# A macaron layer on one NeuronCore: the hand-written orders of five engines and the PSUM banks laid out anew

## The chip, the cores and the metric

The kernel runs on one NeuronCore of a Trainium2 chip. The metric is the device time of one execution in microseconds (us). The engines are TensorE (PE; its weight loads are shown apart as PEld), VectorE (DVE), ScalarE (ACT), GpSimd (POOL) and SyncE (SP), which issues the DMAs.

## What is computed

A half step of a mixture of experts, an attention with low-rank keys and values, and a second half step of the same mixture, each on layer-normed tokens: 4 batches of 1024 tokens, 128 features, 8 experts of which the best two count, 8 query heads on 2 key heads.

```python
def ffn(tokens):                       # router_w (8,128), expert_weights (8,128,128)
    probs = softmax(tokens @ router_w.T + router_b)
    top_p, top_i = top_k(probs, 2)
    w = top_p / (top_p.sum(-1) + 1e-10)
    y_all = einsum('nh,ehd->ned', tokens, expert_weights)
    return (w[..., None] * y_all[top_i]).sum(1)       # then divided by the sum of w
def attn(x):                           # causal, scale 128**-0.5
    q = x @ wq;  k = (x @ wk_down) @ wk_up;  v = (x @ wv_down) @ wv_up
    return softmax(mask(q @ k.T) * scale) @ v @ wo
x = x + 0.5 * ffn(layernorm(x))
x = x + attn(layernorm(x))
x = x + 0.5 * ffn(layernorm(x))
```

## The kernel before

The 4096 tokens are 8 chunks of 512 (two to a batch) and 32 tiles of 128 in each half step, so there are 64 tiles of expert work. The attention of a batch is 4 quads, one for each query chunk and key head, and it goes in slots of 512 score columns: 72 a batch, 288 in all. Every engine runs one long list of steps, written out by hand as a string; one letter is one step, and the n-th time that a letter occurs is the n-th step of its kind. Semaphores carry the order between engines, so a string sets when a step goes and not what it computes. In `PE_ORDER` (line 188) a digit behind a letter is the PSUM bank that the step writes; the loop at line 253 works out from that, for every use of a bank, which earlier use it must wait for (`HOME`; `release`, line 1144, makes the waits). Banks 2 and 3 take scores once the scores have begun, bank 4 takes the weighted values.

The letters, by engine:

- PE: X, x, z transpose a chunk of normed tokens (first half step, attention, second half step); L and l are the router products; Y is half a tile of expert products (three matmuls of 512 columns); K, Q, W project keys, queries and values; M is a block of scores made only to find the row maxima; R turns a quad's maxima into a row; S is a slot of scores; V multiplies weights with values, with the denominators in the same step; J is the output projection of a tile, joined into a chunk; P, U and u prepare weights.
- ACT: E is the exponential of a score slot, C scales one of the first four experts' outputs of a tile (line 734), N, n, m standardise a tile (line 705), X, x, z, K, Q, W, R and O copy from PSUM.
- DVE: M reduces a block of maxima, C adds one of the last four experts (line 991), G is one of 23 steps of routing a unit (line 943), X, x, z take statistics, N, n, m reduce them, I and i make the low part of a transposed chunk, D is one of three steps on denominators, J adds the attention to its input.
- POOL: F is one of three steps that finish a tile of experts (lines 619, 623, 626), N, n, m are one of seven steps of a norm (line 594), A is one running sum of weights over key tiles (line 648; only quads of the second chunk of a batch have them), Y is the product that normalises a quad (line 635).
- SP: K, Q and R stack parts of keys, queries and maxima by DMA, L loads a chunk, O stores one.

Routing and norms of the half steps go by units of one or two chunks: chunk 0, chunk 1, chunks 2 and 3, 4 and 5, 6 and 7 in the first; 0 and 1, 2 and 3, 4 and 5, 6, 7 in the second. The end is thus a chain on the last chunk: V, D, Y on POOL, J, statistics, norm, z, i, l, 23 steps of G, and four tiles of C and F, and a store.

A tile's scaling on ACT and its adding on DVE wait for the tile two before it to be finished on POOL; a slot's exponential waits for the running sums that read the slot 16 before it; V's last group of a quad waits for the quad's sums.

Of the kernel before, what the change touches and what calls it, by code (L numbers as in the profile page):

```python
# [187 lines left out]
PE_ORDER = steps(
    "uX6uL7PPY2X3Y6Y5L3PY7Y2Y6Y5Y7Y2Y6Y5PY7Y3Y2UY6Y5Ux7Q2K3Q1W0X6x5M7M2M3X1L6M7M2M3LM0M1M5M7M2Q3Y0M1W5M7Q5K2M1Y3R"
    "5M7Y5M1M7M1Y6M0SY7SSY1M5M6SY0M5SY7SM1M6SY5M0M1SSM6M0R5V1M5M6M7M0SSY5M6SM7M0SVVM6M7SM0Y5SM6Y7Y0M6SM5VM7SSM6M5"  # L190
    "M1M7V6M5M0SSM1M7Y5Y0R1VM1M5M7VVSSM1x0SY5M6SM7SM1Q0SSK6M7M1SVSM5SM7M0SQ1M5SM6VSM7M0M5SJ6JM7SM0SM5VVSM7SM1M0M5"
    "SM7SJJM1SM0SM5M7W1R0SSVSM5SM0x6M7SM5X0M1SM7V5VSM1M7SX0M6SM1SVL7LSSM6Q0R5SSM1VSK6M0SSM5VM1SY0SY6M5SSW1VVM7SM5"
    "M0SY6M7SY5M1SM0SY7SM6M1SM0SM6Y1M7M0SSM6VV5VM7M0M6SSM7VM0SM6M7SQ5R1SM0SV6M7SJ5JJJM1SSY0M7M1SSM5Y7M1VSM0SY5SM1"
    "SM7M0SY1SVVM7SR0M5V6SM7M0Y5SM1Sz7Y0VVVM7SY5SM1SY6SM0M7Sz1M0SM7Vl5lSM1Y0M7SSJ1JSM7SJJSM7Y6SM1M7SVVSx1M0SM7SM6"
    "Q0SM1M7K6Q1VVM0SY6SM1SM7W0X1M5SY7SR5Y0SM5M7V6SM1SM5Y7VVM1M5M7SSx0Y6M1Y5M0M7Y1Y6SSY5M0M7SM1Y6SY0K7X1Y5M6SVL1L"
    "Y7M0SSQ6SY0SM5VVSR5M7Q6Y0SSM5W7Y6M5Y7SM0VSM5Y1M6SM0SY5SY6M7M1SM0SY7SM1Y5SR0M1VM6M1SSM5M7M0SY6M1SM5M7SY0SM1M5"
    "SV6VVM7SM1SM5Y0SSM6Y7Y1SM5SM6Y0M5SSJ6JJJM5M7SM1M6V5VVVM7M1R6SSY0M5M6SM7M1Y5Y6Y7SSM0M1V0M5Sz6SM1M5SVVVM1SM6SM"
    "5x7z0M1M6SSK7SM5l0lM1SSQ6VVM5SSJ6JSM1SM5JJSSY7M1SQ5VM1SY0M6SM5SY1M6SM5SY7SM6SW5R0SM6VVM5SY7M1SM6SM0Y5SM1M6SV"
    "0VSY1M7SSM6VSM7Y5Sx0M1SM6M5SM0SQ7R1M6SSK5VVSM0Y1SSM5M6Y0VVSM7SM5Y6SM7SM1M5M0SVM7SM1SY5SM0M7Q6R1M0SSY7M0SM6M5"
    "SM0SM1Y6SM5SY0M1SM5SY7SM1M5M6SV1VVSM5SM6M1M7SV5M0SM6M1SM7J0JJJM6SSM1M7M0VR6SM1SM6SM7VVSM0M1SM6M7SV0SSM1M5z6S"  # L200
    "z7M1SM5SVl1lSM6M7SM5VVM6SSW7SM5Y0SSM7M6VVSSM5J7JSM6SJJM5M1SM6SY7SY5SY1R6SY0VSSVSSVSY7SSY5SY6SSV1SSY0VSSVSSz7"
    "Y5SSVSSVl7SSVSSVSSVSSV1VVY0Y6Y2Y5Y3J1JJJY0Y6Y2Y5Y1Y3Y7Y0z6Y2l1Y5Y6Y3Y7Y0Y2Y1Y5"
)
DVE_ORDER = (
    "XXXXNNwwXwXwXXwNwwNIwHGGGGGGGGGGGGXGXGXGXGXGIXGXGXGGNGNGCGGCGCGGCGGGGCCCCGGGGCGCGCGCGGCGGGCGCCGxxCxCCCxnnCPX"
    "CPCPCCCCCPxCCPCCXxxXPxPnnQXKXQXIXMMMIMGGMGMGGMGMGMGMGMGGGMGGQGQGMGRGMGGGMGMGKCMCCCCMCCCMMCCCCMMxMMMCMCXRMCCM"
    "MMMMCxCxCMMMCMMMMxCCCCMMDMnMnNMNMMMMMBCCCDRCMMDMDxMDxMCCMMDMCCMQxMMKMMMxMMMMMnQnMMMXMMMMMBMMRJXMMMMMXMMIMMMI"
    "DMXGGGMDQGzGGRGGGGGGMGMKMMGGGGGGGGGGMCzCCCMMMMzCCMMMMMCMCDCMzMCXMCMMxMXMDXCXDMMNDMQRMxMMJzMMCzzzMMmCmCCMMMNB"
    "MxDMDCRxnCMCCMMDnCCiMCDCDMDMMMCCixCMMMMGGGGMCJMGCGGGMCCxMGCMGMMGzGMxGQGGGKGQGxnGnMGMGGMGMMBCCCRCIMMMCCMCCDMM"
    "MMCCCCMCMCCCMMMCCCCCIKMGCCGMGGGCGGGGMCzGCQGCCGGRGMQGMGGGGGMCCGCGGCMDMCMCCCMMMCCCMMCxCCMCCRMMMxMMMMMMMCCDCCzD"  # L210
    "xDMMzDMCMMMCCMCCCJzxMMnzzzMnmMCBCmDRMMMMMDMCCCMCCCMDMMiMCCxDMMMxDiMDMGxGGGGMQGGMGGMKMMGGGGGGGGxGMGGGnGGJQMMM"
    "MCMBCCCMCnCCCMRMMMMzCCMMMCCzDMCCCCMMMMMRKzMMQCDCMCMMMCMMzMMMMCCMMCMQCMRMMMMCMCMCMCCMMMCCDDCMDMMDMMMMMJzzzzBm"
    "mMMRMMMMMMMDDMDMMMMiiMGMGMMGGGDGGDGGMGDMGGGMGGMGGGGGMGGGMJMMMCCCBCzCCRzzzmmCCCCCCiGDGCDGGGCGCGCGGGCGCDGGGCGG"
    "GCDDDGGCCCGCCCCCGJzzzzCmGmCGCCCCCCCCCCiCCGGGGGCGGCGGCGGGGGGGGGCGGGCGCGCCCCCCCCCCCCCCCC"
)
# [1180 lines left out]
```

## Time and profile before

| | |
|---|---|
| time, median of 3 runs | 460.53 us (459.79 to 461.60) |
| profiled execution | 460.24 us, of which its span is 458.0 us |
| mean granted clock of TensorE in it | 0.987 |
| busy: PE, DVE, ACT, POOL | 420.1, 376.5, 331.6, 315.4 us |
| weight loads (PEld) | 203.1 us |
| DMA, mean over the span | 32 GB/s |

Busy time is the union of an engine's instructions; matmuls overlap one another, so the start of one and the start of the next tell more than their lengths. A stretch's granted clock is the share of TensorE's full speed, 2.4 GHz, that it was given; 0.50 is its lower level, 1.2 GHz. A row of a timeline has the start in us from the start of the span, the length, the engine, the line, the operation, what is written and read, and in brackets how long the engine was idle before and what ended that.

### The profile page before, as it was taken

Reading aid. Unit: us, or ns where it says so; the run is one execution under the profiler, and the core shown is the slowest. Engines: PE = TensorE matmul, PEld = TensorE weight load, DVE = VectorE, ACT = ScalarE, POOL = GpSimd, SP = SyncE. Lnnn points to the kernel's source line nnn. Section 1 sums busy time; section 2 is a strip of 40 time slices with the busy share of each in tenths; the row PEclk is TensorE's granted clock in tenths of the full one; section 3 lists DMA queues with packets and bytes.
Section 4 is the critical chain, followed back from the end, with each engine's and each line's share of the span. In section 5 each row is a group of like instructions: output and inputs, shape, how many; then the busy total and the mean of one; then the engine's idle time right before and its main releaser. Section 6 shows DMA issues by size and latency. Waiting matters only on the chain. (4 is left out here: it accounts for less than half of the span.)

```text
span 458.0 us, 9994 instructions
## 1 busy us (share of the span) xinstructions
PE 420.1 (92%) x3233; PEld 203.1 (44%) x3233; DVE 376.5 (82%) x1199; ACT 331.6 (72%) x749; POOL 315.4 (69%) x413
## 2 busy tenths in 40 slices
...
DMA packets 21123, 14.51 MB, mean 32 GB/s; under 512 B 2952, under 2 KB 20944, under 8 KB 21072
## 3 DMA queue, kind: packets, MB, share of 16 engines
...
q14 instruction: 25, 0.20, 0.2%
...
## 5 line engine op out<-in xcount | busy, mean ns | idle before, releaser
L769 ACT ACTIVATE prob<-bank,exp_scale 128x512 f32<-128x512 f32 x288 | 190.9, 690 | 49.4 <-PE bank L1296 35.9
L648 POOL TENSOR_TENSOR sums<-sums,prob 128x1024 f32<-128x1024 f32 x48 | 112.4, 2359 | 0.1
L1291 PE MATMUL bank<-q_stack,k_stack 98*128 98x512 f16 (+3 forms) x384 | 104.2, 327 | 1.9 <-DMA q_stack<-mT_lo 1.8
L1268 PE MATMUL bank<-k_stack,q_stack 96*128 96x512 f16 (+3 forms) x384 | 101.5, 329 | 2.2 <-DVE m_fin L1007 1.1
L734 ACT ACTIVATE scaled<-bank,gate 128x128 f32<-128x128 f32 x256 | 80.9, 373 | 25.5 <-POOL x L626 10.1
L1011 DVE TENSOR_REDUCE m_part<-bank 128x1 f32<-128x512 f32 x128 | 83.4, 674 | 4.7 <-PE bank L1268 4.3
L619 POOL TENSOR_TENSOR pair_sum<-dve_sum,scaled 128x256 f32<-128x256 f32 x64 | 46.5, 727 | 55.9 <-DVE dve_sum L991 51.0
L1007 DVE CUSTOM_DVE_ANT_0 masked<-bank,mask_qk 128x384 f32<-128x384 f32 (+1 forms) x128 | 76.0, 614 | 6.2 <-PE bank L1268 5.9
L1313 PE MATMUL bank<-prob,v_lat 128*32 128x512 f32 (+3 forms) x768 | 79.0, 494 | 0.2
L1291 PEld LDWEIGHTS bank<-q_stack,k_stack 98*128 98x128 f16 x384 | 36.3, 98 | 54.9 <-ACT prob L769 24.9
L1268 PEld LDWEIGHTS bank<-k_stack,q_stack 96*128 96x128 f16 x384 | 34.9, 98 | 45.0 <-issue 12.3
L1221 PE MATMUL bank<-we_hi,xT_hi 128*128 128x512 f16 x128 | 49.1, 384 | 3.3 <-DVE dve_sum L991 2.2
L705 ACT ACTIVATE xn<-x,shift,half_rstd 128x128 f32<-128x128 f32 x96 | 43.3, 493 | 12.1 <-POOL shift L594 11.2
L1222 PE MATMUL bank<-we_lo,xT_hi 128*128 128x512 f16 x128 | 48.9, 382 | 0.0
L1223 PE MATMUL bank<-we_hi,xT_lo 128*128 128x512 f16 x128 | 48.8, 381 | 0.0
L991 DVE SCALAR_TENSOR_TENSOR dve_sum<-bank,gate,scaled 128x128 f32<-128x128 f32 x128 | 40.7, 339 | 3.8 <-ACT scaled L734 3.6
L648 POOL TENSOR_TENSOR sums<-prob 128x1024 f32<-128x1024 f32 x16 | 37.7, 2360 | 5.2 <-ACT prob L769 5.0
L1296 PE MATMUL bank<-mask_kq,ident_b 128*128 128x256 bf16 (+1 forms) x160 | 40.3, 252 | 0.0
L1318 PE MATMUL bank<-prob,ones 128*32 128x384 f32 (+3 forms) x448 | 37.9, 410 | 0.0
L635 POOL TENSOR_TENSOR yT<-o_sb,r_t 128x512 f32<-128x512 f32 x16 | 20.4, 1275 | 22.9 <-DVE r_t L1046 15.0
L991 DVE SCALAR_TENSOR_TENSOR dve_sum<-bank,gate,x 128x128 f32<-128x128 f32 x64 | 21.8, 341 | 14.0 <-PE bank L1223 9.4
L1313 PEld LDWEIGHTS bank<-prob,v_lat 128*32 128x32 f32 x768 | 18.2, 108 | 32.3 <-issue 23.4
...
## 6 DMA issues: line engine op xcount, KB each, us to landing
...
```

What stands on the lines that cost most here:

```text
L648: nc.gpsimd.tensor_tensor(into, first if j == 1 else into, new, ALU.add).then_inc(sum_step, 1)
L734: nc.scalar.activation(scaled[:, tile % NTB, i, :], home_of(("y", f, n, 2 * t))[:, i * D:(i + 1) * D], ACT.Copy, scale=gate_of(f, n, t)[:, ...
L769: nc.scalar.activation(prob[:, n % NP, :], bank[ST + n % NST][:], ACT.Exp, scale=exp_scale[:, 0:1]).then_inc(p_ready, 1)
L991: V.scalar_tensor_tensor(out=sums[e % 3], in0=home_of(("y", f, n, 2 * t + 1))[:, e * D:(e + 1) * D], scalar=gate_of(f, n, t)[:, HALF + e:H ...
L1007: V.tensor_tensor_reduce(out=masked[:, m % 2, 0:w], in0=seen[:, 0:w], in1=mask_qk[:, CH - w:CH], op0=ALU.add, op1=ALU.max, scale=1.0, scal ...
L1011: V.reduce_max(into, seen[:, 0:w], AX.X).then_inc(mx_red, 1)
L1221: mm(into[:], hi, we_hi[:, cols(half)], start=True, stop=False)
L1222: mm(into[:], hi, we_lo[:, cols(half)], start=False, stop=False)
L1223: mm(into[:], lo, we_hi[:, cols(half)], start=False, stop=True).then_inc(y_done, 1)
L1268: last = mm(into[:, n * w:(n + 1) * w], q_stack[0:MROW, c, g * NR + r, (i % TC) * P:(i % TC + 1) * P], k_stack[0:MROW, b % 2, g, k:k + w], ...
L1291: last = mm(into[:, at:at + CH - off], k_stack[:, b % 2, g, j * P:(j + 1) * P], q_stack[:, c, g * NR + r, off:CH], start=at == 0, stop=not ...
L1313: last = mm(bank[OB][r * DL:(r + 1) * DL, off:CH], v_lat[:, b % 2, j, g, :], weights[r], start=first, stop=final, skip_group_check=True)
```

## The change

All five strings are replaced, PE's with its banks; nothing else is touched. Each letter occurs as often in each string as before (1482 steps on PE, 1058 on DVE, 744 on ACT, 398 on POOL, 116 on SP). The ends of the strings, and POOL's whole, are:

```diff
--- before.py
+++ after.py
 PE_ORDER = steps(
-    "uX6uL7PPY2X3Y6Y5L3PY7Y2Y6Y5Y7Y2Y6Y5PY7Y3Y2UY6Y5Ux7Q2K3Q1W0X6x5M7M2M3X1L6M7M2M3LM0M1M5M7M2Q3Y0M1W5M7Q5K2M1Y3R"
-    "5M7Y5M1M7M1Y6M0SY7SSY1M5M6SY0M5SY7SM1M6SY5M0M1SSM6M0R5V1M5M6M7M0SSY5M6SM7M0SVVM6M7SM0Y5SM6Y7Y0M6SM5VM7SSM6M5"
...
-    "SM0SM1Y6SM5SY0M1SM5SY7SM1M5M6SV1VVSM5SM6M1M7SV5M0SM6M1SM7J0JJJM6SSM1M7M0VR6SM1SM6SM7VVSM0M1SM6M7SV0SSM1M5z6S"
-    "z7M1SM5SVl1lSM6M7SM5VVM6SSW7SM5Y0SSM7M6VVSSM5J7JSM6SJJM5M1SM6SY7SY5SY1R6SY0VSSVSSVSY7SSY5SY6SSV1SSY0VSSVSSz7"
-    "Y5SSVSSVl7SSVSSVSSVSSV1VVY0Y6Y2Y5Y3J1JJJY0Y6Y2Y5Y1Y3Y7Y0z6Y2l1Y5Y6Y3Y7Y0Y2Y1Y5"
+    "uX6uL7PPY2Y3X6PL5Y7Y6Y2Y3PY7Y6Y2Y3UY7Y6Y5Ux1Y2K3Q0Y1Y7Q6W2X5M3M0M1M7M6M5M3M0M1M7M6M2x5K3Q0R5M1X7W6M5M0Q6M7SS"
+    "M1M5M0SM7L1M5SSM0LM7M5V0SM7SR5M6SM7M5SM6SVM7M5SM6VM7SSM5VSM6M7M5SSM0M6V7M5M0SM6SY5M0SM1Y6M0M5M1VM0SY5M1Y6Y0R"
...
+    "M0M5SM7M1SM6SM0V5VVVSM7SM1M6R0SM5SM7SJ1M6SSM0JJSSM5M7M6SJSM0SM5M7SV1SSM6M0M5l7lSM6SM0VVSM5M6SVM0SSM5VSSM6VSM"
+    "0J1M5SSM6M0JSJJSSY5Y6R0SSVSSY7Y1SSVSY0SSY5SVSSY6J1JSY7SY0V5VVSY6SJVSJz7SSY5VSSY6Y0SSY7z1SY6Y5SSVl1lSSVVSSV0V"
+    "VY7Y2Y3Y6Y5J0JJJY1Y7Y2z3Y6Y0l5Y1Y3Y7Y2Y6Y0Y1z3Y2Y7l5Y6Y3Y0Y1Y2Y7Y6Y3Y0Y1Y2Y5Y7"
 )
 DVE_ORDER = (
-    "XXXXNNwwXwXwXXwNwwNIwHGGGGGGGGGGGGXGXGXGXGXGIXGXGXGGNGNGCGGCGCGGCGGGGCCCCGGGGCGCGCGCGGCGGGCGCCGxxCxCCCxnnCPX"
-    "CPCPCCCCCPxCCPCCXxxXPxPnnQXKXQXIXMMMIMGGMGMGGMGMGMGMGMGGGMGGQGQGMGRGMGGGMGMGKCMCCCCMCCCMMCCCCMMxMMMCMCXRMCCM"
...
-    "MCMBCCCMCnCCCMRMMMMzCCMMMCCzDMCCCCMMMMMRKzMMQCDCMCMMMCMMzMMMMCCMMCMQCMRMMMMCMCMCMCCMMMCCDDCMDMMDMMMMMJzzzzBm"
-    "mMMRMMMMMMMDDMDMMMMiiMGMGMMGGGDGGDGGMGDMGGGMGGMGGGGGMGGGMJMMMCCCBCzCCRzzzmmCCCCCCiGDGCDGGGCGCGCGGGCGCDGGGCGG"
-    "GCDDDGGCCCGCCCCCGJzzzzCmGmCGCCCCCCCCCCiCCGGGGGCGGCGGCGGGGGGGGGCGGGCGCGCCCCCCCCCCCCCCCC"
+    "XXXXNNwwXXwwXXNwwNwIHwGGGGGGGGGGXXGGGGGGGXGXGGGXXGXGCICCCGGGGPCCCCxCGCGCCGPGxXCCCCGGGGxGNGGNGGGxnGnGGGGCCCCP"
+    "PXCPPxCCXCCPCCCKXQCCCCxQxxXnnIMMMMMMMMMMMMKRQIMMMMMMMMMGMGMGMGGQGMGRMXMGXGMGGGMGMMMGMGXGMGDMMMGMGMGGMGMGMMMC"
...
+    "MMMRMMMMMMMDMMMRMMMMMMMMMDMMDMMMMMMMDDMMMBDMMMRMDMMDMMMJMMMMMzMGMMGMzGGMGGMGGGMGGDGMGMGGGGMGMMzGzGGDMGGBJCDR"
+    "CzCzzCzmmCCCCCCCCCCCCCCCDDCiCJzCCCizzCzGGGGGCGGCGGGGCGCDGGCGGGmGGCCGmDDGDGGCCCCCCCCJzzzzCmCCCCmiCCCGGGCGGGGC"
+    "GCGCGGGCGGCCCGGCGGCGCGGCGCGCCiCCGGCGCGCGGGCGCCGCGGGGCGCGCGCGGCGGGCCGCGCCCCCCCCCCCCCCCC"
 )
 ACT_ORDER = (
-    "NNNNXHNNNNPLPXCCCCCCPLPCCCCCCCCCCCCCCCCCCCCCnnnCnCCPCCxNQKNQNNnnnnXNNNNXWxQWLQKRCCCCCCCECEECCCCECECCCEECCCCR"
...
-    "EOERKEQECECCEEECEECCCEECEEQREECEEECECECEECECCEEOCEEEEEEREEmEmmmEOmmEEmmEEEzzEEEEEEWElOEEEEECECECEECCCECCREEE"
-    "CCECEECEECEEECmCEEmCEEmmEEOEEzEECCCEElCEEEEEEOCCCCCCCCCCCCCCCCmmmmCCzCCCCCCCCClCCCCCCCCCCCCCCCCC"
+    "NNNNXHPNNPLNNXCCCCPPCCCCCCCCCCLCCCCPCCnnnnCCxCCCCCKCQNCCNCCQNNXnnnnWxNNNKNRQXWQEEEEEEERLEEEEEEEOEEEECCCCCCEC"
...
+    "EEREEEEEEEEEEEEEOEEEEEREEOEEEEEEEEEEEEEEOlEEEEEEEEEECRCEECCEECCCECEECEEECCCECECCmmCmEECmmCmOCEEmECzECECEEmEE"
+    "CCEzCECECClEECEECCCOCCCCCCCCmmmmCCCCzCCCCCClCCCCCCmmCCmmCCCCzCCCCCCCCCClCCCCCCCCCCCCCCCCCCCCCCCC"
 )
 POOL_ORDER = (
-    "NNNNNNNNNNNNNNNNNNNNFFFFFFFFFFNFFFnFnnnnFnnFFFFFFFFFnnnnnnnFFFFFFFFFFFFNnFnFFNnnNFnFFnnNFFNFYNYNFAFFAnAnnnnn"
-    "nAAAAAAAAAFFAFAAYFAFNNFYmFFmmFFmNFNmmFNnmNFFnYnnnFFYnFnNAFAFAFFAFAFFAAnnnAnnFnFnFFFFFFFFFFAFFFAFFFAAFFFAFFFA"
-    "FFFFFFAFFAYFFFFYnFmFFnmmnnnmmmmFnFnFFYFFFFYFAAAAAAnFFnnFFnFnnFnAAAFFAFFFFAAAAFFFFFFAAFYFFFYmmmmmmmYFFAAAAYAA"
-    "AFFFAFmmmFmmFmFmFAAFAAAAAFAFYFFFYFFFFFFFmmmmmmmFFFFFFFFFFFFFFFFFFFFFFFFFFF"
+    "NNNNNNNNNNNNNNFFFFFFFFFFFFnnnnnnnNNFNFNNFNFFNFFFFFFFnnnnnnnFFFFFFYFFFFFNFNAANnnnnnFNnFNnFNAFAFFFNAFAFAAFFFYn"
+    "nnnnnnAAAAAAAAYFFFFNFFYFFNNFFFFnnYnNnnnmnmmAFmmmmFFAAANNFFNFAFAYFFFFFAAnnnnnnnAAAAYFFFAFFFFFFFFFFFFAFFFAFFFF"
+    "FFAFFFFFFFFFFFFnnYnnnnnFFFFFFFFmmFFFFnnnnmnnnYmmmAmAAAAAAYAAAAAAAAAYYYAAAAAAAAYFmFmFmmmFmFmFAFFAFFAFFAFAFAFF"
+    "AFmFAFmFYFFmFmFmYmmFFFFFmFmFmFmFFmFmFFmFFFFFFFFFFFFFFFFFFFFFFFFFFFFFFFFFFF"
 )
 SP_ORDER = (
-    "LLQQQKKKQQQRQQRKQQQQKKRRLRRQLQQKQKQKRRQQKKQQKRRQRQQRRRQKQQKQKRRQQRQQKKQKRQRRQQRRKQOQQKKOQQQRRRKKKQQOQRQRRQQR"
-    "RRROOOOO"
+    "LKKQQQKQQQRRQKKQQKLRQRQQRRLRRKKQQQKLQQQKQQKQKRRQQRQRRRQKKQQKRQRQQRKKQKQQRORRRRQQQQOKKRRQQKQQKQKQKQQRRQRQQRRR"
+    "RROOOOOO"
 )
```

## Rows read from the trace of the kernel before

**Rows 1.** Page: busy us, share of the span, instructions.

```profile
PE 420.1 (92%) x3233; PEld 203.1 (44%) x3233; DVE 376.5 (82%) x1199; ACT 331.6 (72%) x749; POOL 315.4 (69%) x413
```

**Rows 2.** Stretches: length, busy us of PE, PEld, DVE, ACT, POOL, clock, DMA.

```profile
48.00:71.00 23.00, 19.51 (x115) 8.89 (x115) 21.02 (x76) 11.40 (x29) 3.24 (x6) 0.95 0.27 53
71.00:378.00 307.00, 305.55 (x2437) 149.90 (x2434) 272.03 (x787) 239.60 (x518) 213.03 (x250) 1.00 0.10 25
378.00:430.00 52.00, 51.34 (x449) 22.09 (x447) 30.71 (x112) 40.66 (x87) 51.30 (x44) 1.00 0.04 12
430.00:455.20 25.20, 14.54 (x83) 7.02 (x83) 17.73 (x74) 13.76 (x46) 20.18 (x41) 0.96 0.07 21
```

**Rows 3.** Timeline of PE, the end: start, length, line, operation.

```profile
425.52 1.07 PE L1324 MATMUL bank<-sums,ones 128*32 128x512 f32 x8 [0.34 <-POOL sums L648]
...
426.52 0.39 PE L1221 MATMUL bank<-we_hi,xT_hi 128*128 128x512 f16 x1
...
427.18 0.38 PE L1221 MATMUL bank<-we_hi,xT_hi 128*128 128x512 f16 x1
...
430.12 2.02 PE L1335 MATMUL bank<-wo_lat,yT 128*128 128x128 f32 x16 [0.19 <-POOL yT L635]
...
438.25 0.63 PE L1193 MATMUL bank<-ident,xn 128*128 128x128 f32 x4 [0.93 <-ACT xn L705]
...
438.71 0.38 PE L1221 MATMUL bank<-we_hi,xT_hi 128*128 128x512 f16 x1
...
440.53 0.24 PE L1209 MATMUL bank<-xT_hi,rw_hi 128*32 128x128 f16 x4 [1.01 <-DVE xT_lo L833]
```

**Rows 4.** Timeline of POOL, the end.

```profile
379.27 4.71 POOL L648 TENSOR_TENSOR sums<-prob 128x1024 f32<-128x1024 f32 x2
...
428.70 1.27 POOL L635 TENSOR_TENSOR yT<-o_sb,r_t 128x512 f32<-128x512 f32 x1
...
433.86 0.20 POOL L594 TENSOR_TENSOR diff<-stats 128x4 f32<-128x4 f32 x1
...
436.22 0.20 POOL L594 TENSOR_TENSOR shift<-neg_mean,half_rstd 128x4 f32<-128x4 f32 x1
...
451.67 0.72 POOL L619 TENSOR_TENSOR pair_sum<-dve_sum,scaled 128x256 f32<-128x256 f32 x1
...
453.42 0.72 POOL L619 TENSOR_TENSOR pair_sum<-dve_sum,scaled 128x256 f32<-128x256 f32 x1
...
454.75 0.45 POOL L626 TENSOR_TENSOR x<-pair_sum,dve_sum 128x128 f32<-128x128 f32 x1
```

**Rows 5.** Groups by shape: the power steps of the norms, busy, mean ns.

```profile
L594 POOL TENSOR_TENSOR half_rstd<-variance,half_power 128x4 f32<-128x4 f32 x12 | 12.2, 1017 | 0.5
...
L594 POOL TENSOR_TENSOR half_rstd<-variance,half_power 128x8 f32<-128x8 f32 x6 | 9.9, 1646 | 0.3
```

**Rows 6.** Timeline of DVE, the last routing.

```profile
441.92 0.19 DVE L943 TENSOR_TENSOR bank<-bank,g_r 128x32 f32<-128x32 f32 x1
...
442.02 0.34 DVE L991 SCALAR_TENSOR_TENSOR dve_sum<-bank,gate,scaled 128x128 f32<-128x128 f32 x1
...
442.28 0.18 DVE L943 SCALAR_TENSOR_TENSOR bank<-bank,rank 128x32 f32<-128x32 f32 x1
...
446.25 0.24 DVE L943 SCALAR_TENSOR_TENSOR gate<-g_l,y_unit,bank 128x32 f32<-128x32 f32 x1
```

**Rows 7.** Timeline of ACT, a tile of the last chunk.

```profile
446.57 1.14 ACT L734 ACTIVATE scaled<-bank,gate 128x128 f32<-128x128 f32 x4 [3.26 <-DVE gate L943]
```

**Rows 8.** Timeline of PE, the head.

```profile
37.37 0.63 PE L1193 MATMUL bank<-ident,xn 128*128 128x128 f32 x4 [0.95 <-ACT xn L705]
...
40.35 1.97 PE L1232 MATMUL bank<-aT,down_k 128*64 128x512 f32 x2
...
48.00 0.61 PE L1268 MATMUL bank<-k_stack,q_stack 96*128 96x128 f16 x4
...
66.89 0.39 PE L1291 MATMUL bank<-q_stack,k_stack 98*128 98x512 f16 x1 [0.62 <-DMA q_stack<-mT_lo]
```

**Rows 9.** Stretches of the head, columns as in rows 2.

```profile
34.00:38.00 4.00, 1.87 (x10) 0.91 (x8) 2.45 (x9) 3.56 (x12) 3.69 (x8) 1.00 0.01 2
...
40.00:42.00 2.00, 2.00 (x3) 0.29 (x2) 1.38 (x6) 0.69 (x1) 1.27 (x7) 0.50 0.38 113
```

More of the change, by code:

```diff
@@ L188 @@
 PE_ORDER = steps(
-    "uX6uL7PPY2X3Y6Y5L3PY7Y2Y6Y5Y7Y2Y6Y5PY7Y3Y2UY6Y5Ux7Q2K3Q1W0X6x5M7M2M3X1L6M7M2M3LM0M1M5M7M2Q3Y0M1W5M7Q5K2M1Y3R"
-    "5M7Y5M1M7M1Y6M0SY7SSY1M5M6SY0M5SY7SM1M6SY5M0M1SSM6M0R5V1M5M6M7M0SSY5M6SM7M0SVVM6M7SM0Y5SM6Y7Y0M6SM5VM7SSM6M5"
-    "M1M7V6M5M0SSM1M7Y5Y0R1VM1M5M7VVSSM1x0SY5M6SM7SM1Q0SSK6M7M1SVSM5SM7M0SQ1M5SM6VSM7M0M5SJ6JM7SM0SM5VVSM7SM1M0M5"
-    "SM7SJJM1SM0SM5M7W1R0SSVSM5SM0x6M7SM5X0M1SM7V5VSM1M7SX0M6SM1SVL7LSSM6Q0R5SSM1VSK6M0SSM5VM1SY0SY6M5SSW1VVM7SM5"
-    "M0SY6M7SY5M1SM0SY7SM6M1SM0SM6Y1M7M0SSM6VV5VM7M0M6SSM7VM0SM6M7SQ5R1SM0SV6M7SJ5JJJM1SSY0M7M1SSM5Y7M1VSM0SY5SM1"
@@ L194 @@
[L194 to L198, printed above, removed]
@@ L199 @@
-    "0VSY1M7SSM6VSM7Y5Sx0M1SM6M5SM0SQ7R1M6SSK5VVSM0Y1SSM5M6Y0VVSM7SM5Y6SM7SM1M5M0SVM7SM1SY5SM0M7Q6R1M0SSY7M0SM6M5"
-    "SM0SM1Y6SM5SY0M1SM5SY7SM1M5M6SV1VVSM5SM6M1M7SV5M0SM6M1SM7J0JJJM6SSM1M7M0VR6SM1SM6SM7VVSM0M1SM6M7SV0SSM1M5z6S"
-    "z7M1SM5SVl1lSM6M7SM5VVM6SSW7SM5Y0SSM7M6VVSSM5J7JSM6SJJM5M1SM6SY7SY5SY1R6SY0VSSVSSVSY7SSY5SY6SSV1SSY0VSSVSSz7"
-    "Y5SSVSSVl7SSVSSVSSVSSV1VVY0Y6Y2Y5Y3J1JJJY0Y6Y2Y5Y1Y3Y7Y0z6Y2l1Y5Y6Y3Y7Y0Y2Y1Y5"
+    "uX6uL7PPY2Y3X6PL5Y7Y6Y2Y3PY7Y6Y2Y3UY7Y6Y5Ux1Y2K3Q0Y1Y7Q6W2X5M3M0M1M7M6M5M3M0M1M7M6M2x5K3Q0R5M1X7W6M5M0Q6M7SS"
@@ new lines @@
+    "M1M5M0SM7L1M5SSM0LM7M5V0SM7SR5M6SM7M5SM6SVM7M5SM6VM7SSM5VSM6M7M5SSM0M6V7M5M0SM6SY5M0SM1Y6M0M5M1VM0SY5M1Y6Y0R"
+    "1VM5Y1M6Y0Y5SSVM6SY1SM0M5SY7M6SSM0VSM5SM6M0SY1SM5Y7M6SM0SVSM5SM6M1M0SY5SM6SY1M0M7SVM6M0M7SSM6Y5SY0M7SM6M1Sx7"
+    "VR6SSK1Q7Q6SSW1SVV7VSSM6M1M0M5SM6SVSM1M0SM5X6M1SSM0VVM5SM1SM0x6M5M7SM1SM6K0Q5M7SM1VSM6M0SQ5X7M1SJ6JR0SSL7LVV"
+    "M5M0SSJJR1SM5SM0M6SM1SM5V0SM6SM1M5SVVM6SM1M5M0SM6SY1SM5SM0W7M6Y5SM7Y0M6SM1M5SY7SM6M0Y1SY5SSM6M0M7V6VVVM1M0R5"
+    "M7SSM6Y1M5SY0M7SM6SY5M7SJ6JJJSM1M0SM5M7SY1M0SSM6V5VSM7SM0M6VVSx7SM1M0SY6M7M1Y0SSM5Q7K1SM5VSY6SM7M5Y1SM7SQ0z5"
```

23 lines of the change are left out of this document (14 added, 9 removed).

## The prediction

> **What bounds the kernel now.** I read the busy shares first, then the same shares cut into stretches, then the single instructions of the stretches that carry the end, one engine at a time. TensorE (PE) has 420.1 of 458.0 us [rows 1], and between 71 and 378 us it is busy 305.55 of 307.00, while VectorE (DVE) has 272, ScalarE (ACT) 240 and GpSimd (POOL) 213 [rows 2]. Expert products start 0.22 us apart there, three to a step, so a Y step costs 0.65 (426.52 to 427.18, [rows 3]). Between 378 and 430 us POOL is at 51.30 of 52.00 and PE at 51.34: two engines are full [rows 2]. From 430 to 455.2 nothing is: PE 14.5, DVE 17.7, POOL 20.2 of 25.2 [rows 2]. So there are three regimes. A head up to 71 us, in which PE does 19.51 of the last 23 us and DVE 21.02 [rows 2]. A middle that PE alone sets. An end that begins at the first sum of the last batch's third quad (379.27, [rows 4]): POOL and PE go side by side to the first join of the last chunk (430.12, [rows 3]), which I call J, and then a chain of latencies and POOL's tiles lead to the last output tile at 454.75 + 0.45 = 455.20 [rows 4]. The span ends 2.8 us later (the last store), and the profiled execution's time lies 2.24 above its span (460.24 against 458.0). Its median is 460.53, so the profiled one is 0.3 below it; the sum is made against 460.24.
>
> **The rule on busy shares.** TensorE's busy share counts overlapped instructions, which is why I looked at starts: they are 0.22 apart with no gap. The Trainium skill, "Perfetto Trace Analysis", section Identifying the Most-Contended Engine, says that matmul busy time says little and that weight loads should be read instead; by these TensorE has 44% and DVE, at 82%, would be the fullest engine [rows 1]. By that rule the work that goes behind J counts on DVE; DVE has by my count 8.6 us less ahead of its last denominators, where PE has 7.2 less, and the sum below would be 1.4 smaller, 460.1. The trace speaks against it: DVE idles 35 us of the 307 in the middle [rows 2]. That result lies within the forecast's own range, and I give it 0.1 of the forecast's chance.
>
> **The change, part by part.** No instruction is added or removed: I counted the letters of the five strings, and each occurs as often in both. What differs is what stands ahead of what. Where I say by count, I add up an engine's letters up to a place in its string, each at the distance from its start to the next step's start as the trace of before shows it where nothing waits (0.65 for a Y, 0.22 to 0.34 for an S, 1.0 for a V of full width, 0.60 for an M on DVE, 0.26 for a C).
>
> *Work moved behind the last weighted values.* After the last V, PE has 22 Y, 4 J, one z, one l before; 32 Y, 4 J, two z, two l after. Ten Y at 0.65, one z at 0.46 (438.25 to 438.71) and one l at 0.25 [rows 3] make 7.2 us. In a stretch where PE is full, J would come 7.2 sooner, at 422.9.
>
> *POOL ahead of J.* J needs the last yT of POOL (428.70 and 1.27 long, [rows 4]), and POOL is full from 379.27 on. The first sum there is released by a score; PE's work ahead of that score is 14.2 us less after (it has fewer Y ahead of it), so it starts at 365.1. From it to the end of the last yT, POOL needs 50.7 before (379.27 to 429.97). After, there are 10 F steps more (24 against 14) and five norm steps more (12 against 7). A tile of three F steps takes 1.75 (451.67 to 453.42, [rows 4]), so ten take 5.85. Seven norm steps of one chunk take 2.56 (433.86 to 436.42, [rows 4]); a norm of two chunks has a power step of 1.65 in place of 1.02 [rows 5], and the five more, with the exchange of which unit is inside, come to 1.7. Thus 58.3, the last yT ends at 423.4 and J is at 423.5. That is 0.6 later than PE alone would have it; I take POOL's figure.
>
> *From J to the end.* Before, this takes 25.1 (430.12 to 455.20). POOL's own part in it is 34 F (19.9) and 7 norm steps (2.56), less 0.15 by which yT ends before J: 22.3, so POOL waits 2.8. After, it has 48 F (28.1), the last two norm steps of chunk 6 (1.3) and 7 norm steps of chunk 7 (2.56): 31.8 without any wait. The chain: shift is ready after 13 F and those nine norm steps, at J + 11.3. From shift to the l step took 4.1 before (436.42 to 440.53, [rows 3, 4]); after, ACT has two and four scalings more in between (four take 1.14, [rows 7]), part of them while it would wait anyway, which I put at 1.0 to 1.5, so l is at J + 16.4 to 16.9. From l to the gate took 5.96 before (440.53 to 446.49) with 8 combining steps between the 23 gate steps; after there are 17. A gate step and a combining step together take 0.36 (441.92 to 442.28), where gate steps alone stand 0.22 apart, so each of the 9 more costs 0.14 to 0.26: 7.3 to 8.3 [rows 6]. From the gate to POOL's last tile it is 8.7 as before (four tiles are left in both). Together 32.4 to 33.9, above POOL's floor of 31.8; I take 32.7, near the floor, because POOL is fed by 23 combining steps between J and chunk 7's low transpose, where there were 12.
>
> *The head.* After, the second routing unit of 8 tiles (23 gate steps) waits until the first rows of maxima are through, and 3 of the 16 Y of the first two chunks stand behind the first normed transpose x. DVE's work up to the first low row (R) falls from 44.6 to 39.5 by count, and PE's ahead of the first score from 37.8 to 34.2. But the first maxima still wait for the chain x, K, Q, stacking DMAs (37.37 to 48.00, [rows 8]), which no count shortens; the walk through it puts x 0.9 sooner and the first maxima within 1 us of before. Then DVE is the full engine up to about 105 us, as it was from 48 on, and what counts is DVE's work up to a block of maxima plus PE's work from what that block releases. The largest such sum is 415.5 before (71.0 and 344.5) and 414.4 after (59.3 and 355.0): 1.1 gained. Against it, PE stands at the first score for its row's DMA with only four blocks of maxima queued ahead of it, and DVE runs dry for about 1. I put the head at 0, between -2 and +2.
>
> *A tangle of POOL early.* Between the yT of quads 0 and 1, POOL has one norm step before; after, 18 F, 8 sums and 14 norm steps, about 36 us, while PE has 16 us of work between the ends of those quads. The output copy of quad 2 and the first V of quad 3 queue behind that yT. DVE feeds these F steps until about 112 us by its own count, so POOL ends the second yT near 126 us, and that V is due at 127. Price 0.3, between 0 and 2. The DMA order on SP loads chunk 4 first and stacks keys ahead of queries; the six issues that the first maxima need are the same six, so nothing. The banks: the smallest distances from a bank's use to its next use are as short after as before on every kind I compared, so nothing either, up to 1 us.
>
> **The sum.** 423.5 + 32.7 + 2.8 + 2.24 + 0.3 = 461.5, 1.0 above the median.
>
> **Rivals.** First, *slower*: POOL is asked to work from 365 to 456 us without a pause, 91 us, where before it was full for 50. If it waits as in the end of before (2.8 and not 0.9, thus 1.9 more), and the early tangle costs 1.5, the time is 461.5 + 1.9 + 1.2 = 464.6. For it: every wait of POOL past 365 goes straight to the end. Against it: the interleaved order of F and norm steps feeds POOL better than the block of seven before. It decides from a POOL idle time of 2.2 us past 365 on. Second, *faster*: J at PE's 422.9, the end at POOL's floor 31.8, the head at -2, no tangle: 457.8. For the head's part: PE is at the lower of its two levels, 1.2 GHz, granted 0.50, in 40 to 42 us, after a stretch in which it was busy 1.87 of 4.00 us [rows 9], and K, there, takes 1.97 [rows 8]. The three Y now stand in that gap, and at the upper level x to maxima would be some 2 us shorter. The Trainium skill, "TensorE: Matmul & The Clock Gate", Part 1, has the throttled state as the default, which activity lifts; by this the Y would help, and the sum would be 459.5 by that alone. Against it: PE still idles ahead of x, in both orders, as it waits for the norm of the first chunk. Third, that the change doesn't do what it says: the counts of letters exclude it.
>
> **How the numbers follow.** What a measurement of this kernel can tell from no change is about 0.5%, 2.3 us: 458.2 to 462.8. The forecast, 461.5, lies inside, with 459.5 to 463 as its own range; chance 0.47. The slower rival and what is between gives 0.33 above 462.8, the faster one 0.20 below 458.2. Taking the bounds of head (2 either way), tangle (+1.7), end (-0.9, +1.2) and the rivals' ends: 457.3 to 464.8.
>
> **What would show it.** In the profile after: the last V ends near 419.5, J near 423.5; POOL's first sum of the last batch near 365; gate 7 near 447.5, the last tile near 456. If the head is right, the first score is near 60 (66.89 before, [rows 8]) though PE is not ahead by that much at 110. It would be wrong if POOL idles past 365, if the clock stays up between 38 and 50, or if PE shows waits of over 2 us in total between 110 and 365.

## The result, and the profile after

The changed kernel takes **469.22 us** (median of 4 runs, 467.55 to 470.10), the kernel before 461.03 beside it: a ratio of 1.0178, 95% interval 1.0144 to 1.0211. It is slower by 1.8%; the forecast was 461.5, in a range of 457.3 to 464.8. The profiled execution is the slowest of the four, 470.1 us with a span of 467.9, so what the trace shows adds up to 0.9 more than the median does.

The busy line of the page, and TensorE's granted clock in 40 slices of 11.7 us:

```profile
PE 424.5 (91%) x3233; PEld 205.2 (44%) x3233; DVE 376.2 (80%) x1199; ACT 331.6 (71%) x749; POOL 315.8 (67%) x413
...
PEclk9997798999999999999999999999999999999997
```

The instructions are the same (PE has 944 steps; the 1482 named with the change count the bank digits too), and DVE, ACT and POOL are busy as long as before [rows 1]. PE is busy 4.4 us longer, and the clock line shows the likely reason: in slices 4, 5 and 7 it is down to 0.7 and 0.8. The stretches (length, busy us of PE, PEld, DVE, ACT, POOL, clock, DMA), the last two cut at POOL's first sum of the last batch (375.84), at J and at the last tile's end:

```profile
48.00:71.00 23.00, 18.04 (x110) 9.22 (x114) 18.00 (x54) 10.55 (x22) 2.08 (x7) 0.83 0.29 57
71.00:378.00 307.00, 300.41 (x2372) 144.97 (x2368) 261.22 (x750) 232.30 (x492) 204.86 (x228) 1.00 0.10 26
375.84:433.50 57.66, 56.73 (x496) 25.48 (x489) 37.69 (x139) 44.72 (x102) 56.77 (x56) 1.00 0.03 9
433.50:465.10 31.60, 22.00 (x129) 10.46 (x129) 25.47 (x114) 20.57 (x70) 28.46 (x57) 0.96 0.10 29
```

Against [rows 2]: the middle, which PE alone sets, was filled to 305.55 of 307.00 and is now filled to 300.41. From 48 to 71 us DVE has 18.00 of 23.00 where it had 21.02, so it isn't the full engine there any more. The end looks as forecast: POOL 56.77 of 57.66, then 31.60 from J to the end.

Where PE stood still, by its timeline (in brackets, how long it idled and what ended that), and two rows of the chain from J on, J itself and the step l:

```profile
49.85 0.58 PE L1268 MATMUL bank<-k_stack,q_stack 96*128 96x128 f16 x4 [2.15 <-DMA k_stack<-k_lo]
...
68.78 0.59 PE L1268 MATMUL bank<-k_stack,q_stack 96*128 96x512 f16 x2 [2.24 <-DMA k_stack<-k_lo]
...
130.85 0.38 PE L1268 MATMUL bank<-k_stack,q_stack 96*128 96x128 f16 x4 [1.18 <-DMA k_stack<-k_lo]
...
325.00 0.61 PE L1291 MATMUL bank<-q_stack,k_stack 98*128 98x512 f16 x2 [1.79 <-DMA q_stack<-mT_lo]
...
327.54 0.38 PE L1268 MATMUL bank<-k_stack,q_stack 96*128 96x128 f16 x4 [0.85 <-DMA k_stack<-k_lo]
...
337.55 0.38 PE L1268 MATMUL bank<-k_stack,q_stack 96*128 96x128 f16 x4 [1.05 <-DMA q_stack<-q_hi]
...
433.50 2.02 PE L1335 MATMUL bank<-wo_lat,yT 128*128 128x128 f32 x16 [0.85 <-POOL yT L635]
...
448.78 0.24 PE L1209 MATMUL bank<-xT_hi,rw_hi 128*32 128x128 f16 x4 [0.35 <-DVE xT_lo L833]
```

Ahead of J, PE waits for a DMA that stacks keys, queries or a row of maxima; these are the six longest. The view of waits adds all of them up (us in total, times, longest); after, and then before:

```profile
PE bank L1268 <- DMA k_stack<-k_lo: 6.4, 4, 2.2
...
PE bank L1291 <- DMA q_stack<-mT_lo: 2.9, 3, 1.8
...
PE bank L1268 <- DMA q_stack<-q_hi: 1.5, 2, 1.1
```

```profile
PE bank L1291 <- DMA q_stack<-mT_lo: 1.8, 2, 1.1
...
PE bank L1268 <- DMA k_stack<-k_lo: 0.2, 1, 0.2
```

10.8 us in nine waits, against 2.0 in three. And the clock of the head after (columns as above): it is at its lower level, 1.2 GHz, in 36 to 43, 50 to 56 and 70 to 73 us.

```profile
36.00:43.00 7.00, 6.20 (x14) 2.44 (x15) 3.81 (x15) 4.32 (x13) 5.65 (x12) 0.53 0.00 1
43.00:50.00 7.00, 3.84 (x23) 2.43 (x22) 4.34 (x14) 4.41 (x11) 4.54 (x12) 0.96 0.67 121
50.00:56.00 6.00, 6.00 (x26) 3.39 (x25) 5.10 (x16) 1.91 (x5) 0.40 (x2) 0.50 0.18 22
70.00:73.00 3.00, 3.00 (x16) 0.66 (x9) 1.74 (x6) 0.00 (x0) 0.00 (x0) 0.50 0.00 0
```

Each of these stretches follows on one in which PE did little: ahead of the second it was busy 3.84 of 7.00 us, with the wait of 2.15 for the first stacks in it. The time is then paid twice, once as the wait and once as slow work behind it.

**Where the 10.6 us lie.** A step of weighted values (V) is a fixed mark in both orders; the eighth starts here, after and before:

```profile
98.88 0.42 PE L1313 MATMUL bank<-prob,v_lat 128*32 128x256 f32 x4
```

```profile
97.51 0.40 PE L1313 MATMUL bank<-prob,v_lat 128*32 128x256 f32 x4
```

J comes 3.4 us later (430.12 to 433.50) although, by the count of the prediction, PE has 7.2 us less to do ahead of it; so it loses 10.6 us more than before. The same subtraction at other steps places them: +5.9 up to the eighth V (97.51 before, 98.88 after, with 4.5 less work ahead), +6.1 up to the 56th (291.24 and 295.23), +11.5 up to the 72nd (357.46 and 355.77), +10.6 at J. So 5.9 in the head, next to nothing in the 200 us behind it (where the wait of 1.18 at 130.85 stands against one of 1.1 for a row that only the kernel before has), 5.4 between 291 and 357, around the three waits at 325 to 338, and 0.9 given back from there to J.

### The profile page after: what moved, and what is told of

Its sections match the earlier page's. It is cut to its first block, busy times and chain, and to the rows that moved or that the text cites. A ratio compares the mean times of both kernels' runs of the same rounds, so it can differ in the third digit from the quotient of the medians.

```text
span 467.9 us, 9995 instructions
## 1 busy us (share of the span) xinstructions
PE 424.5 (91%) x3233; PEld 205.2 (44%) x3233; DVE 376.2 (80%) x1199; ACT 331.6 (71%) x749; POOL 315.8 (67%) x413
## 4 chain that ended last, share of the span: by engine, by line
PE 59%; POOL 11%; issue 8%; DVE 6%; ACT 5%; DMA 5%; SPq 4%; POOLq 0%; ACTq 0%; DVEq 0%
PE bank L1268 13%; PE bank L1291 11%; PE bank L1313 10%; PE bank L1318 4%; POOL sums L648 4%; PE bank L1221 3%; PE bank L1222 3%; PE bank L1223 3%; SPq L526 3%; DMA k_stack<-k_lo 3%; PE bank L1296 2%; POOL pair_sum L619 2%; ACT scaled L734 2%; PE bank L1335 2%; PE bank L1193 2%
## 5 line engine op out<-in xcount | busy, mean ns | idle before, releaser
L769 ACT ACTIVATE prob<-bank,exp_scale 128x512 f32<-128x512 f32 x288 | 189.2, 689 | 57.5 <-PE bank L1296 35.7
L1268 PE MATMUL bank<-k_stack,q_stack 96*128 96x512 f16 (+3 forms) x384 | 100.0, 335 | 8.1 <-DMA k_stack<-k_lo 6.4
L734 ACT ACTIVATE scaled<-bank,gate 128x128 f32<-128x128 f32 x256 | 79.5, 372 | 28.9 <-PE bank L1223 11.5
L1007 DVE CUSTOM_DVE_ANT_0 masked<-bank,mask_qk 128x384 f32<-128x384 f32 (+1 forms) x128 | 75.0, 615 | 7.2 <-PE bank L1268 6.6
L623 POOL TENSOR_TENSOR pair_sum<-pair_sum 128x128 f32<-128x128 f32 x64 | 29.1, 454 | 3.9
```

What stands on the lines that cost most here:

```text
L734: nc.scalar.activation(scaled[:, tile % NTB, i, :], home_of(("y", f, n, 2 * t))[:, i * D:(i + 1) * D], ACT.Copy, scale=gate_of(f, n, t)[:, ...
L769: nc.scalar.activation(prob[:, n % NP, :], bank[ST + n % NST][:], ACT.Exp, scale=exp_scale[:, 0:1]).then_inc(p_ready, 1)
L1007: V.tensor_tensor_reduce(out=masked[:, m % 2, 0:w], in0=seen[:, 0:w], in1=mask_qk[:, CH - w:CH], op0=ALU.add, op1=ALU.max, scale=1.0, scal ...
L1268: last = mm(into[:, n * w:(n + 1) * w], q_stack[0:MROW, c, g * NR + r, (i % TC) * P:(i % TC + 1) * P], k_stack[0:MROW, b % 2, g, k:k + w], ...
```

## Experiments

Two theories. **Theory 1**: PE's waits for stacks reach the end, and part of them is SP's order alone. **Theory 2**: most of the head's 5.9 is the lower clock. The rivals are those of the prediction: DVE sets the pace of the head and POOL the end, and PE's waits are cover.

**SP's order alone** (`after_sp`), one stretch of SP's string in the order in which its steps become ready:

```diff
-...RORRRRQQQQOKKRRQQKQQKQKQKQQRRQRQQRRR"
+...RORRRRQQQOKKKKKKQQRRQQQQQQQRRQRQQRRR"
```

> The changed kernel with one stretch of SP's string put in the order in which its steps become ready: the keys of chunks 6 and 7 ahead of the queries of chunk 6, and the row of quad 11 inside them. Nothing else differs. Theory 1 (TensorE really loses the 4.1 us that it waits for stacking DMAs at 325.0, 327.5 and 337.6 in the changed kernel, and they reach the end): slot 190 starts at 322.5 to 323.5, block 228 waits for nothing, the join J comes 2.5 to 4 us sooner (433.5 becomes 429.5 to 431), and the time is 465 to 467. Rival (these waits are cover for something else, or POOL's backlog sets J): the waits go, but J stays within 1 us of 433.5 and the time within 1 us of 469.2. A third theory, that the clock of the head makes the whole loss, also expects 469.2 here.

466.17 us, ratio 1.0106 (1.0090 to 1.0121). Slot 190 starts at 322.77 and J comes at 429.75 (433.50), as theory 1 has it; the rival falls.

```profile
429.75 2.02 PE L1335 MATMUL bank<-wo_lat,yT 128*128 128x128 f32 x16 [0.83 <-POOL yT L635]
```

Of these 3.75 us, 0.6 lie ahead of the eighth V (98.30 here), where nothing was edited: they are the difference between two executions. The other 3.2 agree with the 3.05 between the medians. SP's timeline shows the mechanism, first in the changed kernel, then with the edit:

```profile
318.43 0.55 SPq L526 DMA_DIRECT2D q_stack<-q_hi  x1
319.02 0.59 SPq L538 DMA_DIRECT2D out_x<-x  x1
319.72 1.20 SPq L515 DMA_DIRECT2D k_stack<-k_hi  x2
320.96 0.59 SPq L533 DMA_DIRECT2D q_stack<-mT_hi  x1
321.60 0.60 SPq L533 DMA_DIRECT2D q_stack<-mT_lo  x1
322.24 1.81 SPq L526 DMA_DIRECT2D q_stack<-q_lo  x1
324.09 0.61 SPq L526 DMA_DIRECT2D q_stack<-q_hi  x1
324.74 0.60 SPq L515 DMA_DIRECT2D k_stack<-k_lo  x1
```

```profile
299.35 1.20 SPq L515 DMA_DIRECT2D k_stack<-k_hi  x2
300.60 0.60 SPq L515 DMA_DIRECT2D k_stack<-k_lo  x1
...
318.06 0.56 SPq L526 DMA_DIRECT2D q_stack<-q_hi  x1
318.66 0.60 SPq L526 DMA_DIRECT2D q_stack<-q_lo  x1
319.31 0.60 SPq L533 DMA_DIRECT2D q_stack<-mT_hi  x1
319.95 0.59 SPq L533 DMA_DIRECT2D q_stack<-mT_lo  x1
```

The keys of chunk 6 were split by 299.7 and stood for 20 us behind a query that wasn't ready until 318.4. Then nine issues of 0.6 us and more came one behind the other, and the row that slot 190 waited for was fifth and sixth among them.

**The clock alone** (`after_warm`), 40 matmuls that nobody reads, in places where PE waited anyway (in the string, one d each):

```diff
-...UY7Y6Y5Ux1Y2K3Q0Y1Y7Q6W2X5M3M0...M0LM7M5V0...
+...UY7Y6dddddddddY5ddddddUddddx1Y2K3Q0Y1Y7Q6W2ddddX5dddddddM3M0...M0LddddddddddM7M5V0...
+                elif step == "d":
+                    mm(bank[OB][:], we_hi[:, 0:P], we_hi[:, 0:CH], start=True, stop=True)
```

> The changed kernel with 40 matmuls added, whose results nobody reads, in the places where TensorE waits ahead of 69 us: 9 and 6 ahead of the last Y and the second unit step near 33 us, 4 ahead of x, 4 ahead of the transpose of chunk 2, 7 ahead of the first block of maxima, 10 ahead of block 22. They are f16 with 512 columns, 0.22 us each at the upper level of the clock. Theory 2 (of the 7 us that TensorE loses more ahead of 135 us, some 5 come from the lower level of the clock in 36 to 43, 50 to 56 and 70 to 73 us, which follows on its waits): the granted clock stays near 1.00 there, the eighth step of weighted values starts near 94 instead of 98.88, J near 428.5 instead of 433.5, time 463 to 465.5. Rival (the head is held by the stacking DMAs and by DVE, and TensorE has time to spare at either clock): the eighth step of weighted values stays within 1 us of 98.9, and the time is 469 to 470, the added work included.

464.83 us, 1.0070 (1.0055 to 1.0085): 4.4 us gained by added work. The stretches answer to those of the changed kernel above:

```profile
36.00:43.00 7.00, 6.83 (x28) 3.04 (x29) 5.40 (x21) 6.63 (x20) 6.60 (x14) 1.00 0.04 10
43.00:50.00 7.00, 5.71 (x38) 3.22 (x37) 4.15 (x13) 4.00 (x11) 4.06 (x11) 1.00 0.77 132
50.00:56.00 6.00, 4.84 (x22) 2.20 (x23) 6.00 (x19) 3.14 (x9) 0.00 (x0) 1.00 0.00 1
70.00:73.00 3.00, 2.92 (x26) 1.15 (x26) 3.00 (x12) 1.84 (x3) 0.00 (x0) 1.00 0.15 46
```

The upper level throughout, and DVE at 6.00 of 6.00 in 50 to 56, where it had 5.10. The eighth V starts at 94.30 for 98.88. As that step varies by 0.6 between executions with the same head (`after_sp`), the clock of the head cost the changed kernel 4.0 to 4.6 us.

```profile
94.30 0.42 PE L1314 MATMUL bank<-prob,v_lat 128*32 128x256 f32 x4
```

**Both** (`after_sp_warm`).

> Both edits in one kernel: SP's stretch by readiness and the 40 matmuls in the head's gaps. If theories 1 and 2 are both right and the two losses lie one behind the other on TensorE, the gains add up: 459.5 to 463. If only SP's order counts, 465 to 467; if only the clock counts, 463 to 465.5; if POOL sets the end, 468 or more.

461.75 us, 1.0027 (1.0008 to 1.0046). 7.5 less than the changed kernel, where the single edits gave 3.05 and 4.4: by the medians they add up, on one engine, one behind the other. The ten runs spread from 460.34 to 464.05, and the profiled one is the slowest. In it J comes at 426.32, PE's waits for stacks still come to 5.8 us, and the clock is at 0.50 in 440 to 443 us, where J to the last tile takes 32.7 in place of 31.6.

**Which of the added matmuls count** (`after_warm_a`: the 19 ahead of x; `after_warm_b`: the 21 behind it).

> The changed kernel with only the first 19 of the 40 added matmuls, those ahead of x (9, 6 and 4, between 31 and 37 us). Theory 2, split by place: the clock stays up in 36 to 43 us, the first block of maxima starts near 48.0 instead of 49.85, but TensorE still idles from 46 to 48 us for the stacks, the clock still falls behind that, and half of the gain is lost again: eighth step of weighted values 96.5 to 97.5 (98.88 without, 94.30 with all 40), time 467 to 468. Rival (one fall of the clock sets all, and the later ones only follow from it): 94.5 and 465.

> The changed kernel with only the last 21 of the 40, those behind the first keys and queries (4 ahead of the transpose of chunk 2, 7 ahead of the first block of maxima, 10 ahead of block 22). Theory 2, split by place: the first block of maxima stays at 49.85, the stretches 50 to 56 and 70 to 73 us are at the upper level, the eighth step of weighted values is near 96 to 97, time 466 to 467. Rival (as above, the first fall sets all): nothing gained, 98.9 and 469.

468.36 (1.0146, 1.0124 to 1.0167) and 467.23 (1.0131, 1.0108 to 1.0155). The eighth V starts at 96.66 and 96.07, as theory 2 had it; the times are 0.4 and 0.2 above what it gave, and the first one's interval overlaps that of the changed kernel, so its gain rests on the trace. With the first 19, 36 to 43 us is at 1.00, the first block starts at 47.90, and the clock falls all the same, to 0.50 in 48 to 52 us and to 0.52 in 68 to 70, each behind a wait for stacks (2.62 and 2.30 us); with the last 21, 36 to 43 us is at 0.76 and 50 to 56 at 1.00. So the rival, one fall that sets all, is out: each of these stretches follows on an idle time of its own.

**The head on the kernel before** (`head_after`), the changed order up to 60 us on all engines, and then what is left in the order before; too long to show as a diff.

> The changed kernel's steps up to 60 us of its own profile, on every engine, and from there the steps that are left in the order of the kernel before (ten banks had to be renamed). The head alone, then. By the forecast (head 0, between -2 and +2): 459 to 463. Theory 2 (its waits and the lower clock cost 5 to 7 us of TensorE against 2 of the kernel before, and the order before from 60 us on can't hide it): 463.5 to 466, with the granted clock near 0.7 in 36 to 58 us. If DVE, behind by less there, covers half of it: 462 to 463.5.

465.05, 1.0079 (1.0058 to 1.0099), with the clock at 0.77 in 36 to 58 us: the head costs 3.7 us by itself, and the order of the kernel before, behind it, doesn't take that back.

**One part of the change on the kernel before** (`before_sp_late`).

```diff
-...RRQQRRKQOQQKKOQQQRRRKKKQQOQRQRRQQR"
+...RRQQRRQOQQOQQQKKKRRRKKKQQOQRQRRQQR"
```

> The kernel before with one part of the change alone, in its mildest form: the keys of chunk 6 on SP's queue behind the queries of that chunk (three issues moved behind six others), so that their issue slips from 302.6 to about 311 us, where the first block that reads them is due at 312.2. Theory 1 (a stack that lands late stops TensorE, and all of it reaches the end): block 228 waits 2.5 to 3.5 us, J is as much later (430.1 becomes 433), time 463.5 to 464.5. Rival (POOL or DVE has slack that swallows such a wait): J and time within 0.7 of before.

463.39, 1.0051 (1.0027 to 1.0075). In its profiled execution the block starts at 313.75 instead of 312.18, after an idle time of 1.93, and J at 431.66 (+1.5). The direction is theory 1's, the size smaller, since the keys were issued at 310.05 and landed sooner than I took. At the eighth V, ahead of the edit, this execution is 0.5 sooner than the profile of before (96.97 for 97.51), so the edit itself costs J 2.1: what a late stack costs PE is what J loses. The 0.5 shows something else. With the same order of PE the clock is at 1.00 in 46 to 50 us here and at 0.60 in the profile of before, so whether it falls behind a gap differs from execution to execution.

**The added matmuls on the kernel before** (`before_warm`, 21 of them; `before_warm2`, 7 more ahead of the first block of maxima).

> The kernel before with 21 such matmuls in its own gaps between 35 and 47 us (5 ahead of the second unit step, 4 ahead of x, 5 ahead of the first query projection, 3 and 4 ahead of the next two transposes). Theory 2: its two stretches at the lower level, 40 to 43 and 46 to 50 us, go or shrink, the first block of maxima starts 1 to 1.5 us sooner (46.5 to 47 for 48.0), and the time is 459 to 460.3 where it was 461. Rival (DVE is the full engine from 48 us on and covers it): within 0.5 of 461.

> The kernel before with the 21 added matmuls of the earlier run and 7 more ahead of its first block of maxima, where TensorE sat idle from 46.1 to 47.9 us and the clock then went to 0.50 from 50 to 56 us. Theory 2 (an idle stretch is what the fall follows on): the granted clock is 1.00 all through 36 to 58 us. What that is worth here is open: if TensorE set the pace in 50 to 75 us, the eighth step of weighted values starts 1 to 2 us sooner than 97.5 and the time is 459 to 460; if DVE does, as the forecast had it, it stays within 0.7 of 97.5 and the time within 0.7 of 461.2.

The first: 459.88, 0.9984 (0.9954 to 1.0013), no difference that can be told, and its premise failed. The lower level went from 40 to 43 us, and came back later:

```profile
40.00:43.00 3.00, 3.00 (x13) 1.51 (x13) 2.35 (x8) 2.38 (x5) 2.20 (x8) 1.00 0.25 75
46.00:48.00 2.00, 0.22 (x4) 0.13 (x3) 0.76 (x2) 1.65 (x4) 0.00 (x0) 1.00 0.57 153
50.00:56.00 6.00, 6.00 (x35) 1.83 (x24) 5.76 (x23) 1.36 (x4) 0.00 (x0) 0.50 0.00 1
```

PE idled 1.78 of the 2 us ahead of 48, and then ran at 0.50. With 7 more matmuls in that gap, 36 to 58 us is at 1.00, the eighth V starts at 96.43 (97.51), and the time is **459.22**, 0.9964 (0.9951 to 0.9977): faster than both kernels. So in its profiled execution the lower clock costs the kernel before 1.1 us up to there as well. That DVE, busy 16.18 of 17.00 us in 58 to 75, covers what more the clock costs there is likely and not shown.

**A row issued in one piece** (`before_warm2_row`): in two places of SP's string, QQ between the two issues of a row goes behind them (RQQR becomes RRQQ, QRQQR becomes RRQQQ).

> The kernel before with the 28 added matmuls, and two places of SP's string changed: the two issues of a row of maxima (quads 0 and 5) put side by side and ahead of the stacking of queries that stood between them, which are needed later. In the kernel before these rows land at 66.84 and 170.30, and TensorE waits 0.80 and 1.29 us for them ahead of slots 0 and 82. Theory 1: slot 82 starts about 1.3 us sooner against the kernel with the 28 matmuls alone and nothing waits there; J follows by 1 to 1.5; time 457.5 to 458.7 (slot 0 lies where DVE sets the pace, and brings 0 to 0.5). Rival (such a wait is given back by a later one): slot 82 sooner, J and time unchanged, 459.2.

**458.32**, 0.9948 (0.9928 to 0.9967). Slot 82 waits for nothing, where it waited 1.15 us with the 28 matmuls alone, and J comes 0.9 sooner, at 428.23 (429.09); 1 to 1.5 were expected. The rival falls by the trace: slot 82 starts 0.8 sooner, and J keeps it. The two intervals overlap, so by the times alone the 0.9 us are not clear; it is the lowest median here.

**Waits taken out by count** (`before_opt_warm2`), many steps moved on all engines, in fact from 67 us on.

> The same, and past 75 us the orders of the kernel before with steps moved by a few places on all engines so that stacks are issued sooner ahead of the blocks that read them (the waits at slot 82 and block 22), and less stands between the last joins and the last routing. Theory 1 says that what is taken from those waits reaches the end: 1 to 3 us below the kernel with the 28 matmuls alone, 457 to 459.5. If the waits are covered by DVE or POOL, no difference from that one.

470.86, 1.0214 (1.0185 to 1.0244): a plain miss. The steps were moved with every latency taken as fixed, until no wait was left on paper. On the chip block 22 starts at 75.83 (71.21 with the 28 matmuls alone), the clock is at 0.80 in 58 to 75 us with DVE at 12.78 of 17.00, and by the count PE loses a few tenths of a us more in most stretches of 10 us of the middle than the kernel before does. Which of the moves did it was not taken apart.

## Why the prediction was wrong, step by step

**What failed is J's time.** 423.5 was forecast, 433.50 came. The term is "in a stretch where PE is full, J would come 7.2 sooner": the 7.2 us are right, but PE was not full, and two steps of the working let it pass as full: the head put at 0, and the DMA order put at nothing.

*The head, put at 0 between -2 and +2.* It cost 5.9 us of PE up to the eighth V. The lower clock takes 4.0 to 4.6 in the changed kernel (`after_warm`) and 1.1 in the kernel before (`before_warm2`), so some 3 to 3.5 of the 5.9 are clock. With both kernels at the upper level 2.4 remain (94.30 against 96.43, with 4.5 less work ahead); that these are PE's waits for stacks is likely and not shown. The text said that what counts is DVE's work plus PE's behind it, and so priced the clock only as a gain (the faster rival). It had the row for the loss at hand: K at 1.97 and a clock of 0.50 behind a stretch with PE busy 1.87 of 4.00 [rows 8, 9]. The faster rival's "three Y" in the gap behind x are one: two of the three stand behind K and Q. That one ran at the lower level itself, its matmuls 0.43 apart, and so did K and Q:

```profile
38.01 0.63 PE L1221 MATMUL bank<-we_hi,xT_hi 128*128 128x512 f16 x1
38.44 0.63 PE L1222 MATMUL bank<-we_lo,xT_hi 128*128 128x512 f16 x1
...
39.43 1.97 PE L1232 MATMUL bank<-aT,down_k 128*64 128x512 f32 x2
41.33 1.74 PE L1239 MATMUL bank<-aT,aq 128*128 128x512 f32 x2
```

The fall came sooner (36 us), after PE had idled 1.92 and 1.22 us. And the first maxima came not within 1 us of before but 1.85 later: K now goes ahead of Q, the first of the two projections starts at 39.43 instead of 39.17 and takes 1.97 instead of 1.25, SP's first issue for the maxima comes at 42.92 (41.95), and the last of the six lands at 49.76 (47.91). The Trainium skill, "TensorE: Matmul & The Clock Gate", section HAM oscillation — how this bites in real kernels, describes a kernel that waits for a DMA between groups of matmuls, finds the clock down behind each wait, and pays for both. The trace agrees: 0.50 in 50 to 56 and 70 to 73 us, each behind a wait for stacks. The prediction used only the default state of this page, as a rival for a gain.

*"The DMA order on SP ... so nothing".* It looked only at the six issues for the first maxima, and at which they are, not at when they come. Eight more waits of PE for stacks lie behind the one for these, 10.8 us with it, against 2.0 before. Two things make them. One is SP's order, an item that isn't ready holding others that are: 3.05 us by `after_sp`. The other is distance, which I compared for banks and not for stacks. From the start of a key projection to the block that reads it the chain takes 8.9 us in one case (121.93 to 130.85 in the changed kernel: projection, two splits by 124.50, six issues up to 127.78, 3.0 until the last lands). That is the shortest of the eight in the changed kernel; in the kernel before two took 6.0 and 7.6 to the landing of the keys, with SP issuing in another order. Where the order leaves less PE work than that in between, PE stops, whatever it has less to do. The wait of 1.18 at 130.85 is of that kind, and no experiment here moved it; that it would go with an earlier projection is only argued.

*"It would be wrong if PE shows waits of over 2 us in total between 110 and 365".* It shows 5.3. The condition was the right one; the prediction had no case for it, and no chance on it. The range had room for neither loss: its own bounds (2, 1.7 and 1.2) add up to 466.4 above and not to 464.8, and the result lies outside both.

**What held.** POOL's first sum starts 375.84, not 365.1, later by the 10.7 us that PE lost; from there every term is near. To the end of the last yT 57.5 (58.3), and PE waits 0.85 for it at J (0.6). From J to the end of shift 10.4 (11.3), from there to l 4.9 (5.1 to 5.6), l to the gate's end 7.5 (7.3 to 8.3), gate to the end of POOL's last tile 8.8 (8.7): 31.6 in all for 32.7, against 25.1 before. The rows:

```profile
375.84 2.35 POOL L648 TENSOR_TENSOR sums<-prob 128x1024 f32<-128x1024 f32 x1 [0.77 <-ACT prob L769]
...
432.09 1.27 POOL L635 TENSOR_TENSOR yT<-o_sb,r_t 128x512 f32<-128x512 f32 x1
...
443.73 0.20 POOL L594 TENSOR_TENSOR shift<-neg_mean,half_rstd 128x4 f32<-128x4 f32 x1
...
464.62 0.45 POOL L626 TENSOR_TENSOR x<-pair_sum,dve_sum 128x128 f32<-128x128 f32 x1
```

POOL's waits between 375.84 and the end come to 1.0 us, under the 2.2 from which the slower rival decides. So the kernel is slower, but not by that rival's mechanism. The early tangle on POOL cost nothing: the second yT comes at 133.86, for 126 forecast, but PE, late itself, waits nowhere for it. The fall of the faster rival is told above.

**The rule on busy shares.** The Trainium skill, "Perfetto Trace Analysis", section Identifying the Most-Contended Engine, would have DVE as the fullest engine and gave 460.1. The trace speaks against it again: DVE idles 46 of the 307 us of the middle, and what moved the time were edits on PE's gaps and SP's queue that leave DVE's work alone.

With both losses taken away, the changed kernel is at 461.75, beside 461.5 forecast. That this is so close is in part luck: the added matmuls also take away the 1.1 us of clock that the forecast left in, the wait at 130.85 remains, and in the profiled execution J comes at 426.32, not at 423.5.
